# A transformer chain on one core: a feed-forward's first tiles quantised in the attention before it, its weights rounded in another order and place

## What is computed

```python
def int4_quant(x):
    beta = jnp.mean(jnp.abs(x), axis=-1, keepdims=True)
    x_q = jnp.clip(jnp.round(x * SQRT7 / (beta + EPS)), -8, 7)
    return x_q * (beta * SQRT7) / SQRT7
def bitlinear(x, w, scale):
    w_mean = jnp.mean(jnp.abs(w))
    w_q = jnp.clip(jnp.round(w / (w_mean + EPS)), -1.0, 1.0)
    return jnp.einsum('...i,oi->...o', x, w_q * w_mean * scale)
gate, up = bitlinear(int4_quant(x), w_gate, s_gate), bitlinear(int4_quant(x), w_up, s_up)   # 512 -> 1376
return bitlinear(int8_quant(up * jnp.square(jax.nn.relu(gate))), w_down, s_down)            # 1376 -> 512
```

## Time and profile before

| | us |
|---|---|
| three runs | 849.05, 860.44, 857.54 (median 857.54) |
| profiled execution | 855.71 |
| its span in the profile | 853.7 |
| TensorE, VectorE, ScalarE, GpSimd busy | 781.5, 701.0, 532.5, 408.5 |
| mean granted clock of TensorE | 0.972 of full speed |

### The profile page before, as it was taken

How to read it: one execution, slowest core, us unless ns; L and a number is a source line. 1 busy time by engine, 2 the same in 40 slices (tenths; PEclk the granted TensorE clock), 3 DMA queues, 4 the chain that set the end, 5 groups by cost and what they waited for, 6 DMA issues and landing times. The chain is left out here.

```text
span 853.7 us, 16366 instructions
## 1 busy us (share of the span) xinstructions
PE 781.5 (92%) x5150; PEld 638.0 (75%) x5150; DVE 701.0 (82%) x1762; ACT 532.5 (62%) x1441; POOL 408.5 (48%) x374
## 2 busy tenths in 40 slices
PE   1976799858988999999999999999999999999988
PEld 0474576534677898888888888989889888786556
DVE  7878998969787887897897898798888888787855
ACT  6875798745457557657657656665665576772541
POOL 3237078715035844845746646745754663401120
PEclk9999999979999999999999999999999999999879
DMA  8254236544020310320320320320310210004001
GB/s 302 104 172 151 76 127 228 175 125 153 16 84 1 107 69 1 98 74 0 98 74 0 98 74 0 98 71 3 98 49 25 75 50 26 2 0 120 1 1 50
DMA packets 37488, 65.67 MB, mean 77 GB/s; under 512 B 5377, under 2 KB 17729, under 8 KB 37314
## 3 DMA queue, kind: packets, MB, share of 16 engines
q1 hardware_dynamic: 37442, 65.10, 23.2%
HBM read 59.76 MB, written 5.33 MB: 76 GB/s over the span
## 5 line engine op out<-in xcount | busy, mean ns | idle before, releaser
L2428 DVE TENSOR_SCALAR_CACHE_REDUCE xn<-ctxT,candidate 128x512 bf16<-128x512 f32 x240 | 168.8, 741 | 0.0
L2075 ACT ACTIVATE layer_attention_probs<-xnT,stats 128x512 f32<-128x512 f32 x128 | 94.0, 734 | 117.7 <-DVE stats L2217 117.7
L1813 PE MATMUL bank<-layer_attention_keysT,layer_attention_queriesT 128*128 128x512 f32 x384 | 120.9, 423 | 4.7 <-DVE layer_attention_queriesT L2210 4.6
L2229 DVE TENSOR_TENSOR layer_attention_probsT<-bank,layer_attention_probsT 128x512 fp32r<-128x512 f32 x128 | 88.1, 688 | 41.0 <-ACT layer_attention_probsT L2083 39.6
L1813 PEld LDWEIGHTS bank<-layer_attention_probsT,layer_attention_values 128*128 128x128 f32 x768 | 100.2, 191 | 10.9 <-DVE layer_attention_probsT L2229 3.1
L2083 ACT CAST layer_attention_probsT<-bank 128x512 fp32r<-128x512 f32 x128 | 74.8, 584 | 50.4 <-PE bank L1896 50.3
L1813 PE MATMUL bank<-layer_attention_probsT,layer_attention_values 128*128 128x256 f32 x768 | 103.5, 284 | 2.2 <-DVE layer_attention_probsT L2229 1.6
L1813 PE MATMUL bank<-layer_attention_l_wkv,layer_context_parts 128*128 128x256 f32 x720 | 93.7, 283 | 0.0
L1813 PE MATMUL bank<-layer_attention_l_wq,layer_attention_xnT 128*128 128x512 f32 x384 | 93.6, 392 | 0.0
L1813 PEld LDWEIGHTS bank<-layer_attention_l_wkv,layer_context_parts 128*128 128x128 f32 x720 | 91.3, 191 | 2.7
L1813 PE MATMUL bank<-layer_attention_wo,layer_attention_headsT 128*128 128x512 f32 x336 | 88.7, 405 | 0.4 <-ACT layer_attention_squares L2034 0.4
(11 more groups left out here) (347 smaller groups left out, 1673.2 us busy)
## 6 DMA issues: line engine op xcount, KB each, us to landing
layer_attention_l_raw_qo<-in_wqT SPq DMA_DIRECT2D x8, 1024.0 KB, 5.5
layer_attention_l_raw_qo<-in_woT SPq DMA_DIRECT2D x8, 1024.0 KB, 6.5
xnT<-inverse_sums SPq DMA_DIRECT2D x14, 512.0 KB, 3.6
tw_raw<-in_w_gateT SPq DMA_DIRECT2D x8, 688.0 KB, 5.3
tw_raw<-in_w_upT SPq DMA_DIRECT2D x8, 688.0 KB, 4.1
tw_raw<-in_w_downT SPq DMA_DIRECT2D x6, 768.0 KB, 4.7
layer_attention_l_raw_kv<-in_wkvT SPq DMA_DIRECT2D x8, 512.0 KB, 5.0
ternary<-tw_rounded SPq DMA_DIRECT2D x8, 344.0 KB, 2.5
```

Source lines behind the costliest of these rows:

```text
L1813: last = pe.matmul(out, stationary[f][a], moving[f][b], start=f == 0 and x == 0, stop=f == count - 1 and x == 2)
L2075: a.activation(probs[:, u % 3, :], masked[:, u % 2, :], ACT.Exp, bias=negmax[:, u:u + 1], scale=-1.0, accum_out=sums[:, u:u + 1]).then_inc ...
L2229: v.tensor_tensor(probsT[:, 1, p % 2, :, columns], T[u % 2][:, :].rearrange("p (c q) -> p c q", c=CPB), probsT[:, 0, p % 2, :, columns], A ...
L2428: own(k.nc.vector.tensor_scalar((k.flags if flags is None else flags)[:, r % 2], row_tile(k.ctxT, r), k.candidate[:, r:r + 1].bitcast(F32) ...
```

## The change

- Pieces are rounded in another order: gate, down, up. The first nine are stored as before. The last four (up) aren't stored: GpSimd writes them straight to `front.up`, which lies where batch 0's queries were; it first waits until all scores of batch 0 are done.
- The rounded gate weights are read back inside the attention, by three DMAs among the loads of up pieces 1 to 3: chunks 0 and 1 to where `k.xnT` is, chunk 2 to where batch 0's values were, after the mix of batch 0. The six loads into `wgu` are gone.
- ScalarE takes the magnitudes of tiles 0, 1 and 2 in the attention (at u = 60 and after the last unit), that of tile 3 in the feed-forward behind the first square.
- VectorE quantises tiles 0 and 1 at the attention's end; division and addition of the attention's tile 3 are moved to the feed-forward. TensorE turns the two tiles as the attention's last work.
- In the feed-forward VectorE's list is: scales, division and addition, statistics of tile 3, product 0, rows of tile 3, product 1, two passes over tiles 2 and 3, product 2, their codes, scales. After that, each tile's magnitude, scaling and rounding have the next tile's products 0 and 1 between them.
- TensorE's turns of tiles 2 and 3 are behind tile 1's chunks, the turn of tile 0's inner row behind the first chunk of tile 2; ScalarE's copies follow.
- The two bisection counts are VectorE's last work in the feed-forward.

```diff
+    ROUNDED = (0, 1, 2, 3, 8, 9, 10, 11, 12, 4, 5, 6, 7)
+    STORED = 9
@@ ternary_round_gpsimd
-        if i >= 2:
+        if 2 <= i < tw.STORED:
             g.wait_ge(tw.stored[n % 2], 16 * (i // 2))
+        if i == tw.STORED:
+            g.wait_ge(scores_psum, TPB * HEADS1)
+        rounded = tw.rounded[0:rows, n % 2, 0:width] if i < tw.STORED else k.front.up[:, f, :]
@@ ternary_round_sync
+    def gate_load(c, target):
+        source = tw.scratch[GATE].rearrange("(f p) c -> p f c", p=P)
+        sp.dma_start(target, source[:, :, 512 * c:min(512 * c + 512, INNER)]).then_inc(tw.gate_loaded, 16)
+    for i, piece in enumerate(tw.ROUNDED):
+        if 2 <= i < tw.STORED + 2:
             store(i - 2)
+        elif i >= 2:
+            sp.wait_ge(tw.rounded_ready, i - 1)
+        ternary_load(k, piece, count + i)
+        if i == tw.STORED + 1:
+            for p in range(2):
+                sp.wait_ge(tw.stored[p], 16 * (KT // 2))
+            sp.wait_ge(latent_psum, B)
+            gate_load(0, k.front.gate[0])
+        if i == tw.STORED + 2:
+            gate_load(1, k.front.gate[1])
+        if i == tw.STORED + 3:
+            sp.wait_ge(quads_done, TPB * HEADS1 // 4)
+            gate_load(2, k.front.gate[2])
@@ new functions
+def front_magnitudes_scalar(k, n, t):
+    a, r = k.nc.scalar, k.front
+    a.wait_ge(k.tile_xn, TILES * n + t + 1)
+    a.activation(r.x4[:, t, :], k.xn[:, t, :], ACT.Abs, accum_out=r.beta[:, t:t + 1]).then_inc(r.beta_ready, 1)
+def front_rounded_vector(k, own, h):
...
+    for t in tiles:
+        own(v.tensor_scalar(r.t1[:, t % TPB, :], k.xn[:, t, :], SQRT7, r.binv[:, t:t + 1], ALU.mult, ALU.mult))
+    own.wait()
+    for t in tiles:
+        own(v.tensor_scalar(r.t1[:, t % TPB, :], r.t1[:, t % TPB, :], ROUND, ROUND, ALU.add, ALU.subtract))
+def front_codes_vector(k, own, h):
+    own.wait()
+    for t in range(h * TPB, (h + 1) * TPB):
+        v.tensor_scalar(r.x4[:, t, :], r.t1[:, t % TPB, :], -8.0, 7.0, ALU.max, ALU.min).then_inc(r.x4_ready, 1)
@@ layer1_attention, tensor / vector / scalar
                 turn_mixed(TILES - 1)
+                for t in range(TPB):
+                    front_turn_tensor(k, t)
-                divide_mixed(TILES - 1)
-                add_mixed(TILES - 1)
+                front_rounded_vector(k, own, 0)
+                front_codes_vector(k, own, 0)
+                    if u == 60:
+                        front_magnitudes_scalar(k, following, 0)
+                front_magnitudes_scalar(k, following, 1)
+                front_magnitudes_scalar(k, following, 2)
                 copy_mixed(TILES - 1)
@@ layer1_ffn, scalar
+                        if i == 0:
+                            front_magnitudes_scalar(k, n, TILES - 1)
+                        if (t, c) == (2, 0):
+                            x8T_copy(0)
@@ layer1_ffn, vector
-                bisection_count(k, own, 0, first_flags(k))
-                for c in range(NC):
-                    inner_chunk(0, c)
-                    if c == 0:
-                        bisection_count(k, own, 1, first_flags(k))
+                scales(0)
+                attention_update()
+                tile_variance_vector(k, TILES - 1)
+                inner_chunk(0, 0)
+                tile_rows_vector(k, n, TILES - 1)
+                inner_chunk(0, 1)
+                front_rounded_vector(k, own, 1)
+                inner_chunk(0, 2)
+                front_codes_vector(k, own, 1)
+                scales(1)
                 for t in range(TILES):
                     magnitude(t)
+                    if t + 1 < TILES:
+                        inner_chunk(t + 1, 0)
                     scaled(t)
                     if t + 1 < TILES:
-                        inner_chunk(t + 1, 0)
+                        inner_chunk(t + 1, 1)
                     own.wait()
                     rounded(t)
-                    if t + 1 < TILES:
-                        inner_chunk(t + 1, 1)
...
+                for j in range(FRONT_COUNTS):
+                    bisection_count(k, own, j, first_flags(k))
@@ layer1_ffn, tensor
-                gate_up(0)
-                turn4(2)
-                turn4(3)
-                gate_up(1)
+                pe.wait_ge(tw.gate_loaded, 16 * NC)
+                pe.wait_ge(tw.rounded_ready, len(tw.PIECES))
+                gate_up(0, range(NC))
+                gate_up(1, range(NC))
+                for t in range(TPB, TILES):
+                    pe.wait_ge(x4T_ready, t - 1)
+                    front_turn_tensor(k, t)
+                gate_up(2, range(1))
                 turn8(0)
-                gate_up(2)
+                gate_up(2, range(1, NC))
                 down(0)
                 turn8(1)
-                gate_up(3)
+                gate_up(3, range(NC))
```

More of the change, by code:

```diff
@@ L437, in ternary_round_gpsimd, with ternary_round_sync @@
         k.pown.wait()
-        g.tensor_scalar(tw.rounded[0:rows, n % 2, 0:width], raw, -ROUND, 1.0, ALU.add, ALU.mult)\
+        g.tensor_scalar(rounded, raw, -ROUND, 1.0, ALU.add, ALU.mult)\
          .then_inc(tw.rounded_ready, 1)
-def ternary_round_sync(k):
+def ternary_round_sync(k, latent_psum, quads_done):
     tw, sp = k.ternary, k.nc.sync
@@ L446, in store @@
     def store(i):
-        w, f, rows, width = tw.PIECES[i]
+        w, f, rows, width = tw.PIECES[tw.ROUNDED[i]]
         n = count + i
@@ L859, in __init__ @@
         self.high, self.low = k.keep("context_high"), k.keep("context_low")
+class FeedForwardFront:
+    def __init__(self, k, stack):
+        right = lambda name, shape, dtype: k.sbuf("front_" + name, shape, dtype, stack, side="right")
+        small = lambda name, shape: right(name, shape, F32)
+        self.values = right("values", [P, CPB, D], F32)
+        self.queries = right("queries", [P, HEADS1, SEQ], F32R)
+        codes = k.nc.alloc_sbuf_tensor_at("front_codes", [P, HEADS1 * SEQ * 2], BF16, offset=k.nc.sbuf_top)[:, :]
+        self.inverse = small("inverse", [P, HEADS1])
+        self.beta, self.betae, self.binv, self.gate_scale, self.up_scale = (
+            small(x, [P, TILES]) for x in ("beta", "betae", "binv", "gate_scale", "up_scale"))
+        passes = self.values[:, :, :].rearrange("p c d -> p (c d)")
+        chunks = k.xnT[:, :, :].rearrange("p f c -> p (f c)").bitcast(BF16).rearrange("p (n f c) -> p n f c", n=2, c=512)
+        u, x, t, g, w = KT * INNER, TILES * D, TPB * D, KT * (INNER - 1024), KT * P
+        self.up = codes[:, 0:u].rearrange("p (f c) -> p f c", f=KT)
+        self.x4 = codes[:, u:u + x].rearrange("p (t c) -> p t c", t=TILES)
+        self.t1 = passes[:, 0:t].rearrange("p (t c) -> p t c", t=TPB)
+        last = passes.bitcast(BF16)[:, 2 * t:2 * t + g].rearrange("p (f c) -> p f c", f=KT)
+        self.gate = (chunks[:, 0], chunks[:, 1], last)
+        self.x4T = (codes[:, u + x:u + x + w].rearrange("p (f c) -> p f c", f=KT),
+                    passes.bitcast(BF16)[:, 2 * t + g:2 * t + g + w].rearrange("p (f c) -> p f c", f=KT))
+        self.beta_ready, self.x4_ready, self.x4T_psum = (k.keep("front_" + x) for x in ("beta_ready", "x4_ready", "x4T_psum"))
@@ new lines, in front_magnitudes_scalar @@
+def front_magnitudes_scalar(k, n, t):
[3 more added lines that the diff above has]
+def front_rounded_vector(k, own, h):
+    v, r = k.nc.vector, k.front
+    two, tiles = slice(h * TPB, (h + 1) * TPB), range(h * TPB, (h + 1) * TPB)
+    v.wait_ge(r.beta_ready, TPB * (h + 1))
+    own(v.tensor_scalar(r.beta[:, two], r.beta[:, two], 1.0 / D, None, ALU.mult))
+    own.wait()
+    own(v.tensor_scalar(r.betae[:, two], r.beta[:, two], EPS, None, ALU.add))
+    own.wait()
+    own(v.reciprocal(r.binv[:, two], r.betae[:, two]))
+    own.wait()
+    for t in tiles:
+        own(v.tensor_scalar(r.t1[:, t % TPB, :], k.xn[:, t, :], SQRT7, r.binv[:, t:t + 1], ALU.mult, ALU.mult))
+    own.wait()
+    for t in tiles:
+        own(v.tensor_scalar(r.t1[:, t % TPB, :], r.t1[:, t % TPB, :], ROUND, ROUND, ALU.add, ALU.subtract))
@@ new lines, in front_codes_vector, with front_turn_tensor @@
+def front_codes_vector(k, own, h):
+    v, r = k.nc.vector, k.front
+    own.wait()
+    for t in range(h * TPB, (h + 1) * TPB):
+        v.tensor_scalar(r.x4[:, t, :], r.t1[:, t % TPB, :], -8.0, 7.0, ALU.max, ALU.min).then_inc(r.x4_ready, 1)
+def front_turn_tensor(k, t):
+    pe, r = k.nc.tensor, k.front
+    pe.wait_ge(r.x4_ready, t + 1)
+    for f in range(KT):
+        last = pe.transpose(front_turned(k, t)[:, f * P:(f + 1) * P], r.x4[:, t, f * P:(f + 1) * P], k.ident16[:, :])
+    last.then_inc(r.x4T_psum, 1)
@@ L862, in context_split, with front_turned @@
+def front_turned(k, t):
+    return k.bank[(6, 5)[t % 2]][:, 0:256].bitcast(BF16)
 def context_split(k):
@@ L1359, in _, with scales @@
                 own = k.vown
[L1360 to L1365 removed]
+                def scales(h):
+                    two = slice(h * TPB, (h + 1) * TPB)
```

(6 more changed lines are left out.)

146 lines of the change are left out of this document (55 added, 91 removed).

## The result

| | before | after |
|---|---|---|
| median of 20 runs, us | 854.6 (849.05 to 860.44) | 861.94 (856.45 to 865.8) |
| ratio to before, run beside run | 1 | 1.0081 [1.0062, 1.010] |
| profiled execution, us | 855.71 | 860.41 |
| its span, us | 853.7 | 858.7 |
| mean granted clock | 0.972 | 0.970 |

The kernel became 0.8% slower, about 6.9 us, where 0.4% faster was forecast. That is inside the 2%, but over twenty runs of each it can be told from no change, and 861.94 us lies outside the range of 846 to 860.

A forecast was written before the change was run, and what follows sets the result against it. TensorE's idle feed-forward start, VectorE's passes in the middle and TensorE's list at the end were taken as bounds. Attention 0 and feed-forward -3.3 us, from a middle of 856.6, gave 853.3 us; range 846 to 860.

The forecast's parts named there:

- the term for the splits: Feed-forward's start: GpSimd's wq and wkv splits, moved beside VectorE's small passes, cost 1.5 us at most, taken as 0.5.
- the port: Rival, chance 0.03: every VectorE pass next to a split waits 1.8 us, eight times; net +7 us, 863.6.
- Rounding late: Rival, chance 0.12: slow loads of up pieces 1 to 3 delay GpSimd's last piece; net +6 us, 862.6.
- Attention's end: End of attention: block 0.6 us earlier, GpSimd's rounding 0.8 us later, cancelling to 0.2; feed-forward starts at 182.9, as now.
- GpSimd ends 0.8 us later: Attention's rounding in the new order: waits for loads total 8.0 us against 7.2.
- Feed-forward's start: First gate matmul at 183.5 in place of 189.65, 6.2 us sooner; VectorE's first magnitude pass at 195.4, 3.0 us earlier.
- The sum up to the magnitude: Feed-forward's start: VectorE's work and waits ahead of its first magnitude pass add to 12.0 us, before the splits' term.
- Middle: Feed-forward's middle: VectorE's passes stay the same, its 3.0 us shift is carried through; TensorE gains 0.5 more.
- End: Feed-forward's end: TensorE's last down matmuls end at 228.4, 3.5 us sooner; VectorE with the two counts at 228.5.

The follow-up runs named there:

- run 1: Changed kernel, with GpSimd's split of the next layer's weights held back until VectorE has both pairs of scales: median 856.0 us, ratio to the kernel before 1.0019.
- run 5: Kernel before, with four more unused 128x512 subtractions on GpSimd ahead of the splits, beside VectorE's quantising passes: median 859.13 us, ratio 1.0049.
- Run 2: Changed kernel, with VectorE's bisection update moved from unit 55 to unit 61, behind GpSimd's last rounding pass: median 859.53 us, ratio to the kernel before 1.0035.
- run 8: Kernel before, with only VectorE's bisection update moved from unit 55 to unit 61: median 854.23 us, ratio 0.9996.
- run 4: Kernel before, with only the rounding order changed to gate, down, up, all thirteen pieces still stored and loaded: median 856.14 us, ratio 1.0024.
- Run 6: Changed kernel with splits held back and update at unit 61, the two counts moved into VectorE's gaps: median 852.08 us, ratio to the kernel before 0.9971.
- run 3: Changed kernel with both GpSimd's splits held back and the bisection update moved to unit 61: median 853.48 us, ratio to the kernel before 0.998.

## Why the prediction was wrong

The kernel became slower because work of GpSimd came to lie beside short SBUF instructions of VectorE that stand in a chain, at two places.

**The step that failed** is the term for the splits: "Six small passes of this kind at 60% more would be 1.5 us at most ... I take 0.5". The move of the splits was right (issued at 185.39, started at 193.49), the term was 7.2 us (19.26 us from the block's start to the magnitude, 12.05 in run 1). Its unit was wrong. I took a share of VectorE's own duration, from a row in which a pass met only what was left of a GpSimd instruction: 1.51 against 0.94. And that instruction wasn't the split at 201.44, as the prediction has it, but the cast ahead of it:

```profile
200.32 1.04 POOL L1556 CAST layer_attention_l_wkv<-layer_attention_l_raw_kv 128x1024 fp32r<-128x1024 f32 x1 [15.69 <-DMA layer_attention_l_raw_kv<-in_wkvT]
```

The scaling pass started at 200.58 and the cast ended at 201.36: 0.78 us of wait, and 0.94 of work would make 1.72, against 1.51. The row already had the whole wait in it. What counts is the number of VectorE's instructions of the kinds that wait, times what is left of the GpSimd pass beside each; in a chain that is nearly the whole pass, whatever the instruction's size. The three scale operations, 0.2 us each in my sum, cost as much as the passes. The singly timed instructions above read as if each instruction of VectorE that gets through lets the next GpSimd pass in, and the one behind it waits again; no run tests that order by itself.

One row of the kernel before would have shown the size. The timeline has an addition that takes 0.69 us in the earlier trace rows at more than twice its length, beside a rounding pass of GpSimd:

```profile
163.50 1.55 POOL L436 TENSOR_SCALAR tw_raw<-tw_raw,tw_winv 128x1536 f32<-128x1536 f32 x1
164.09 1.50 DVE L1121 TENSOR_TENSOR x<-x,layer_attention_mixed 128x512 f32<-128x512 f32 x1
```

0.69 us of work begun at 164.09 and a pass that ends at 165.05: 0.96 of wait and 0.69 of work would be 1.65, close to the 1.50. The rival *the port* had this mechanism at 0.03, and its step of +7 is the nearest to the measured +6.9. That nearness is in part luck: its price was 1.8 us eight times, and seven instructions waited about 1.0 us each; it hid 4 us of that in waits, which didn't happen. *Rounding late* is as near by its time (862.6), but what it needs didn't occur: GpSimd's scales were early. The Trainium skill ("SBUF — State Buffer", section "Who interferes with whom") says that one engine's instruction "fully blocks" the other, where VectorE runs in a two-port mode or reads two inputs from SBUF. I wrote that the trace agreed in sign and not in size. The seven instructions above and the four of run 5 agree with it in size, and so does, read rightly.

**Attention's end: 0 forecast, +1.5 measured.** "GpSimd ends 0.8 us later" was wrong by sign: 60.4 us from the first pass to the scales, 62.2 before. The gate reads disturbed nothing (a wait of 0.88 us ahead of the first up piece and none ahead of the other three, of which the last is shown):

```profile
153.08 1.48 POOL L440 TENSOR_SCALAR tw_raw<-tw_raw,tw_bound 128x1376 f32<-128x1376 f32 x1 [0.88 <-DMA tw_raw<-in_w_upT]
...
166.63 1.48 POOL L440 TENSOR_SCALAR tw_raw<-tw_raw,tw_bound 128x1376 f32<-128x1376 f32 x1
```

What failed is that I counted only VectorE's edited instructions. The update at unit 55 is in no line of the diff, but full up passes were moved beside it. Run 2 takes the loss away (4.3 us, of which 1.4 is the update's place, run 8); run 4 shows +0.6 of it from the order alone.

**Feed-forward's start.** First gate matmul at 185.38, 4.3 us sooner and not 6.2; behind the block's start it is 1.07 us, against 0.6 forecast and 6.8 before. The granted clock of 184.20 to 190.00 is 0.71, not near 1.00. The sum up to the magnitude, without the splits' term, was 12.0 and is 12.05 in run 1.

**Middle.** "VectorE's shift of 3.0 us is carried through": from the magnitude to the next layer it is 33.86 us before and 33.59 in run 1, so this holds where the magnitude comes early. In the change it is 34.75: from 198.40 to 212.40 the trace grants TensorE a clock of 0.51, over and behind its wait of 7.06 us, where it had 1.00 before. That the clock costs these 1.2 us fits, but no run separates it. Run 6 gives 34.47 by the counts.

**End.** TensorE's last down matmuls end at 234.79 + 2.55 = 237.34, VectorE's counts at 237.71, by this part of VectorE's timeline:

```profile
237.63 0.08 DVE L2509 DVE_READ_ACCUMULATOR xnT<-ctxT,candidate 128x1 f32 x1
238.32 0.75 DVE L2409 SCALAR_TENSOR_TENSOR x<-bank,down_scale,x 128x512 f32<-128x512 f32 x1 [0.60 <-PEq L1385]
```

0.37 us past TensorE, 0.1 forecast: the step was right.

By the traces, then, the feed-forward without its clash is 3.8 us shorter from the block's start to the next layer (runs 1 and 3), where -3.3 was forecast, and the two clashes take +8.4 and about +1.5. The 3.8 depends on the trace that it is set against: this stretch takes 47.61 to 49.43 us where it isn't edited, which makes it 2.0 to 3.8. The times show less than the stretches. In run 3 the feed-forward's 3.8 and the attention's 2.7 us (14.59 against 17.29) would be a gain of 6.5 us, a ratio of 0.9924, but its interval begins at 0.9949. In run 1 the feed-forward's 3.8 less the 0.9 us that the attention's end is longer (18.19 against 17.29) would be 2.9 us, 0.9966, but its interval begins at 0.9993. Where the rest goes stays open, and that the design gains what was forecast is not shown as time. Open are also the 1.0 us that the rest of the program is shorter in the trace of the change, and the 6.9 us of the runs against the 5.0 of the traces.

## What to carry to other kernels

When a change moves a DMA or a wait earlier, ask which GpSimd passes it releases and list VectorE's SBUF instructions at the new time, those that no edit touches included. Price each one of the kinds that wait at nearly one whole GpSimd pass, whatever its size: a chain of seven short ones cost 7.2 us here. The kinds that waited are in the next section. GpSimd work that nobody waits for is put behind a semaphore that VectorE gives at the end of its chain, beside long passes: here one such wait turned 54.0 us of feed-forward into 45.6.

## What was not expected of the hardware

- The smallest instructions lose the most for their length: 128x2 from 0.22 to 1.31 us, 128x8 int32 from 0.17 to 1.31, beside GpSimd passes of 1.25 and 1.34 us.
- The loss goes both ways. Of the next layer's four subtractions on GpSimd, the first and the last take 1.26 us in the kernel before. The middle two begin while a VectorE pass over 1376 columns, which had waited for GpSimd, gets its work done, and they take 1.90. In the change, beside 128x2 instructions, three of them take 1.26 and one 1.32. So the 1.82 a pass of the earlier trace rows has GpSimd's own wait in it. In run 1 the cast beside tile 0's two long passes takes 2.53 us, 1.89 in the kernel before. All four of the kernel before:

```profile
207.00 6.22 POOL L1565 TENSOR_TENSOR layer_attention_l_wq<-layer_attention_l_raw_qo,layer_attention_l_wq 128x512 fp32r<-128x512 f32 x4
207.12 0.15 DVE L1404 TENSOR_SCALAR layer_ffn_gammae<-layer_ffn_gamma 128x1 f32<-128x1 f32 x1
```

- Not every VectorE instruction waits. The kinds that did are TENSOR_SCALAR on two or more columns, and instructions with two inputs outside the banks. The 128x1 instruction in the rows above keeps its 0.15 us inside a subtraction; the products, which read one input from a bank, keep 0.75 beside the splits, and the bisection's counts 0.74. It matters too what GpSimd does. Later in the trace of the kernel before, the update's first operation, on 128x8 elements, takes 2.28 us (at 294.47) beside a GpSimd pass over 1024 columns, and its last keeps 0.17 (at 297.31) beside a GpSimd instruction of 1.01 us on 128x4 elements. In the kernel before, the magnitude pass of tile 1 lies beside a GpSimd cast for 1.4 us and keeps its length; after the change, one codes instruction beside the same cast waits it out (0.38 us when alone, half of the pair's 0.76 in the earlier trace rows). VectorE's and GpSimd's timeline, before:

```profile
205.02 1.89 POOL L1562 CAST layer_attention_l_wq<-layer_attention_l_raw_qo 128x2048 fp32r<-128x2048 f32 x1
205.50 1.59 DVE L1402 TENSOR_REDUCE layer_ffn_gamma<-layer_ffn_inner 128x1 f32<-128x1376 f32 x1
```

  and after (the second codes instruction by itself):

```profile
197.59 2.08 POOL L1643 CAST layer_attention_l_wq<-layer_attention_l_raw_qo 128x2048 fp32r<-128x2048 f32 x1
197.84 2.11 DVE L936 TENSOR_SCALAR front_codes<-layer_front_values 128x512 bf16<-128x512 f32 x1
```
